# Two decays of a selective scan are computed before the convolution's Silu and kept in a free pair of PSUM banks

## What is computed

```python
xc = silu(conv(xs) + conv_b)                 # per channel, over the tokens
delta = softplus(xc @ xd_w @ dtp_w + dtp_b)
Bm, Cm = xc @ xB_w, xc @ xC_w
dA = exp(delta[..., None] * A)               # the decays
dBx = (delta * xc)[..., None] * Bm[:, :, None, :]
h = dA_t * h + dBx_t                         # step by step over the tokens
y = einsum('bdn,bn->bd', h, C_t) + D * xc
out = y * silu(z) @ out_w + res
```

## Time and profile before

| what | value |
|---|---|
| median of three runs | 10367.23 us (10365.20 to 10386.27) |
| profiled execution | 10389.18 us |
| its span | 10387.4 us |
| mean granted clock of PE | 0.87 of 2.4 GHz |
| DVE busy | 8087.7 us (78% of the span) |
| PE busy | 8344.1 us (80%) |
| POOL busy | 7059.5 us (68%) |
| ACT busy | 5899.2 us (57%) |

### The profile page before, as it was taken

How to read it: one execution, slowest core, us unless ns; L and a number is a source line. 1 busy time by engine, 2 the same in 40 slices (tenths; PEclk the granted TensorE clock), 3 DMA queues, 4 the chain that set the end, 5 groups by cost and what they waited for, 6 DMA issues and landing times. The chain is left out here.

```text
span 10387.4 us, 152898 instructions
## 1 busy us (share of the span) xinstructions
PE 8344.1 (80%) x42776; PEld 6881.5 (66%) x42776; DVE 8087.7 (78%) x10482; ACT 5899.2 (57%) x9202; POOL 7059.5 (68%) x7227
## 2 busy tenths in 40 slices
PE   5877777777878787878787877787877776999998
PEld 4666666666666666666666666676666664777776
DVE  4888889888988888888898888888888894333332
ACT  4565656565665666566566666665566662444443
POOL 4888888888888888888888888888888883000000
PEclk8888888888888888888888888888888887999998
DMA  2222222222222222222222222222222220000000
GB/s 93 94 89 99 92 98 91 99 92 93 92 94 93 90 98 93 90 79 90 89 98 93 98 91 97 93 98 92 90 93 96 92 90 25 11 10 10 12 9 9
DMA packets 414916, 819.68 MB, mean 79 GB/s; under 512 B 148919, under 2 KB 194139, under 8 KB 414043
## 3 DMA queue, kind: packets, MB, share of 16 engines
q1 hardware_dynamic: 410328, 806.69, 22.3%
q10 hardware_dynamic: 3714, 2.89, 0.1%
HBM read 783.16 MB, written 26.30 MB: 78 GB/s over the span
## 5 line engine op out<-in xcount | busy, mean ns | idle before, releaser
L776 ACT ACTIVATE decay<-delta,neg_a 128x512 f32<-128x512 f32 x4096 | 2793.0, 688 | 2484.5 <-DVE h_ps L978 1112.7
L544 POOL TENSOR_TENSOR bu<-b_all,u_buf 128x512 f32<-128x512 f32 x3072 | 3579.4, 1191 | 151.6 <-DVE h_ps L978 148.3
L978 DVE TENSOR_TENSOR_SCAN h_ps<-decay,bu 128x512 f32<-128x512 f32 x2304 | 2782.6, 1222 | 454.6 <-ACT decay L776 376.3
L1233 PE MATMUL y_ps<-ident,ch 128*128 128x128 f32 x16384 | 2579.9, 309 | 637.4 <-DVE ch L998 362.7
L1233 PEld LDWEIGHTS y_ps<-ident,ch 128*128 128x128 f32 x16384 | 2226.7, 161 | 1016.2 <-DVE ch L998 484.4
L556 POOL TENSOR_TENSOR ch<-ch,c_all 128x512 f32<-128x512 f32 x1024 | 1325.5, 1294 | 1112.1 <-DVE ch L978 910.0
L998 DVE TENSOR_TENSOR ch<-h_ps,c_all 128x512 f32<-128x512 f32 x3072 | 1977.2, 671 | 0.0
L547 POOL TENSOR_TENSOR bu<-b_all,u_buf 128x514 f32<-128x514 f32 x1024 | 1245.6, 1237 | 66.8 <-issue 56.3
L1117 PE MATMUL w_ps<-xn,in_w 128*128 128x257 f32 x4096 | 1074.8, 408 | 170.5 <-ACT xn L665 83.6
L982 DVE TENSOR_TENSOR_SCAN h_ps<-decay,bu 128x256 f32<-128x256 f32 x1536 | 1046.7, 737 | 125.3 <-POOL bu L547 98.2
L1117 PEld LDWEIGHTS w_ps<-xn,in_w 128*128 128x128 f32 x4096 | 799.9, 206 | 320.2 <-issue 81.1
(11 more groups left out here) (258 smaller groups left out, 11583.9 us busy)
## 6 DMA issues: line engine op xcount, KB each, us to landing
b_all<-bc_dram SPq DMA_DIRECT2D x512, 514.0 KB, 8.6
c_all<-bc_dram SPq DMA_DIRECT2D x512, 514.0 KB, 10.0
in_w<-in_L_attn_in_w SPq DMA_DIRECT2D x64, 1024.0 KB, 5.0
diag_store<-diag_dram SPq DMA_DIRECT2D x256, 256.0 KB, 2.9
x_in<-in_x SPq DMA_DIRECT2D x128, 256.0 KB, 2.6
out_w<-in_L_attn_out_w SPq DMA_DIRECT2D x64, 512.0 KB, 3.9
skip_diag<-skip_dram SPq DMA_DIRECT2D x64, 256.0 KB, 4.1
h_mid<-h_cur SPq DMA_DIRECT2D x32, 257.0 KB, 2.2
```

What stands on the lines that cost most here:

```text
L544: pool.tensor_tensor(bu[:, s % NBU, 0:NB * L].rearrange("p (b t) -> p b t", b=NB), b_all[:, n // NU, n % NU, :, 1:], u_buf[:, c % 2, :, 1: ...
L776: func(decay[:, s % NDP, :].rearrange("p (b t) -> p b t", b=NB), delta[:, c, :, 1:S], ACT.Exp, scale=neg_a[:, k, c, n:n + 1]).then_inc(dec ...
L978: dve.tensor_tensor_scan(h, decay[:, s % NDP, :], bu[:, s % NBU, 0:NB * L], 0.0, ALU.mult, ALU.add).then_inc(scan_done, 1)
L1233: last = pe.matmul(y_ps[:, k, :], ch[:, s % NPR, k * P:(k + 1) * P], ident[:, :], is_transpose=True, start=False, stop=(n == NST - 1 and k ...
```

## The change

A new key "early" stands between cv3 and xp in the list of results, so it has a slot and two of the three banks of `w_ps`. ACT writes the decays of states 52 and 53 (`EARLY`) into these two banks in unit 24, right behind decay 51 and ahead of `token_rows` and the Silu. The decays of 54 and 55 then wait for the scans of 50 and 51 (`behind`). DVE scans 52 and 53 from those banks and counts "early" as read once scan 53 is done. In the last period, which prepares no job, all is as before.

```diff
+EARLY = 2 * (CONV_AT + 9) + 4, 2 * (CONV_AT + 9) + 5
...
-        steps = first + conv + ["xp", "dt0", "dt1", "dt2", "dt3"]
+        steps = first + conv + ["early", "xp", "dt0", "dt1", "dt2", "dt3"]
...
+            def early_decays(g, jj):
+                k = BLOCK_OF_JOB[jj % 4]
+                w = banks("early", g, jj + 1)
+                for c in (2, 3):
+                    act.wait_ge(read_of(f"cv{c}", g, jj + 1), nth(f"cv{c}", g, jj + 1))
+                for i, s in enumerate(EARLY):
+                    c, n = s // NST, s % NST
+                    func(w[:, i, :].rearrange("p (b t) -> p b t", b=NB), delta[:, c, :, 1:S], ACT.Exp,
+                         scale=neg_a[:, k, c, n:n + 1]).then_inc(decays_ready, 1)
+                act.sem_inc(full_of("early", g, jj + 1), 1)
...
-                if positive(job_count(g, jj, STATES, s + 1 - NDP)):
-                    act.wait_ge(scan_done, job_count(g, jj, STATES, s + 1 - NDP))
+                if positive(job_count(g, jj, STATES, s + 1 - NDP - behind)):
+                    act.wait_ge(scan_done, job_count(g, jj, STATES, s + 1 - NDP - behind))
...
             def lead(g, jj, s, last):
+                if not last and s in EARLY:
+                    return
                 if not (last and s >= STATES):
-                    decays(g, jj, s)
+                    decays(g, jj, s, behind=NDP if not last and s - NDP in EARLY else 0)
...
                     lead(g, jj, NU * u + NDP + 1, last)
+                    if NU * u + 2 * NDP in EARLY and not last:
+                        early_decays(g, jj)
                     if u == silu_at(jj)[1]:
                         token_rows(g, jj, u // PAIRS - 1)
...
+            def decay_of(g, jj, s, last):
+                if s in EARLY and not last:
+                    return banks("early", g, jj + 1)[:, EARLY.index(s), :]
+                return decay[:, s % NDP, :]
...
+            def early_read(g, jj):
+                dve.wait_ge(scan_done, job_count(g, jj, STATES, EARLY[-1] + 1))
+                dve.sem_inc(read_of("early", g, jj + 1), 1)
...
                         c_times_h(g, jj, s)
                         if s + 1 not in POOL_C:
                             c_times_h(g, jj, s + 1)
+                    if s in EARLY and not last:
+                        early_read(g, jj)
```

More of the change, by code:

```diff
@@ L762, in stream_out, with decays @@
                 func(dst[:, c, :, :], w[:, :, 0:S], ACT.Identity).then_inc(read_of(name, g, jj), 1)
-            def decays(g, jj, s):
+            def early_decays(g, jj):
[8 more added lines that the diff above has]
+                act.sem_inc(full_of("early", g, jj + 1), 1)
+            def decays(g, jj, s, behind=0):
                 jj, s = on(jj, s)
@@ L819, in prepare_back @@
                     conv_output(g, jj, c + 1)
+                act.wait_ge(read_of("cv3", g, jj), nth("cv3", g, jj))
+                act.sem_inc(full_of("early", g, jj), 1)
+                act.sem_inc(read_of("early", g, jj), 1)
                 conv_silu(g, jj)
@@ L962, in h_slot, with scan @@
                 return len([v for v in range(s) if v not in POOL_C]) % NU
-            def scan(g, jj, s, b):
+            def decay_of(g, jj, s, last):
[5 more added lines that the diff above has]
+                dve.sem_inc(read_of("early", g, jj + 1), 1)
+            def scan(g, jj, s, b, last):
                 inside = s not in POOL_C
@@ L976, in scan @@
                 if s >= NST:
-                    dve.tensor_tensor_scan(h, decay[:, s % NDP, :], bu[:, s % NBU, 0:NB * L], 0.0, ALU.mult, ALU.add
+                    dve.tensor_tensor_scan(h, decay_of(g, jj, s, last), bu[:, s % NBU, 0:NB * L], 0.0, ALU.mult, ALU.add
                                            ).then_inc(scan_done, 1)
@@ L1055, in period @@
                     for b in range(NB if s < NST else 1):
-                        scan(g, jj, s, b)
+                        scan(g, jj, s, b, last)
                     if u - 1 in y_at(jj):
@@ L1062, in period @@
                         step_size(*size, 0)
-                    scan(g, jj, s + 1, 0)
+                    scan(g, jj, s + 1, 0, last)
                     if s + 1 in POOL_C and s < NST:
                         c_times_h(g, jj, s)
-                        scan(g, jj, s + 1, 1)
+                        scan(g, jj, s + 1, 1, last)
                     else:
                         if s < NST:
-                            scan(g, jj, s + 1, 1)
+                            scan(g, jj, s + 1, 1, last)
                         c_times_h(g, jj, s)
```

## The result

| what | before | after |
|---|---|---|
| median | 10366.22 us (4 runs) | 10444.21 us (4 runs) |
| ratio, 95% interval | | 1.0074 (1.0057 to 1.0092) |
| profiled execution, its span | 10389.18, 10387.4 us | 10442.90, 10441.0 us |

The change makes the kernel 78 us slower (59 to 95 us by the interval).

A forecast was written before the change was run, and what follows sets the result against it. VectorE (87% busy up to 8540 us) was taken to bound the kernel. Weighted by the clock, 0.5 x 2.5 + 0.4 x 0.7 - 0.1 x 1.0 = +1.4 us a job, +88 us over 63 jobs: 10455 us, range 10300 to 10520.

The forecast's parts named there:

- ACT's order: On ScalarE, early decays push y_t, table loads and Silu 1.25 us later; decays 54, 55 end at +5.2, +5.8.
- DVE: On VectorE, scan 52 starts at +0.63, output(2) waits 0.7 us for y2, scan 54 starts 2.6 us earlier.
- The wait for the banks: On TensorE, xp needs the early decays' banks and starts at +4.8, after scan 53, instead of +1.98.
- The rival of a longer wait: The count of "early" waits for product 52, xp starts at +5.4: +2.1 us a job, 10500 us, chance 0.17.
- The Ln as the end of the path: VectorE waits 0.58 us for the first Ln at a job's end; a job gains what that Ln gains.
- The sum with the clock up: With TensorE's clock staying at full rate, the Ln and the job come 1.0 us earlier; 63 jobs gain 65 us.
- The clock: TensorE's clock falls to 1.2 GHz behind idle stretches of 2.25 and 2.3 us, turning the gain into +1.4 us a job.
- The kinds of jobs: Per job: clock stays up -1.0 us; falls only behind second idle stretch +0.7; falls behind the first +2.5.
- The weights: Shares of jobs: one in ten clock up, four in ten fall behind second stretch only, half fall behind the first.
- The clock holds: Rival: TensorE's clock stays up in this stretch, -1.0 us a job, 10302 us, chance 0.15.
- Only xp is hit: Rival: only TensorE's second idle stretch brings the clock's fall, +0.7 us a job, +44 us, 10411 us, chance 0.13.
- The loads for the next job: The store of B and C goes out 0.5 us later, with 7 us of cover before the first reader: costs nothing.

The follow-up runs named there:

- e1: Changed kernel with TensorE given zero-matrix products in both idle stretches, before the skip products and before xp, all waits kept: 10309.92 us, ratio 0.9941.
- e2: Changed kernel with the two early decays in an SBUF buffer and the key "early" removed, so xp waits for the Silu alone: 10274.92 us, ratio 0.9905.
- e6: Changed kernel with only TensorE's second idle stretch, ahead of xp, filled with products that add zeros: 10330.69 us, ratio 0.9958.
- e9: Changed kernel with the key "early" and its bank wait kept, but decays 52 and 53 back in their old place and buffers: 10635.21 us, ratio 1.0260.
- e3: Changed kernel with ScalarE's copy y_t ahead of the two early decays instead of behind them: 10339.98 us, ratio 0.9964.
- e7: e3 with TensorE's adds of states 50 and 51 also moved ahead of xp: 10294.60 us, ratio 0.9924.
- e5: Changed kernel with only TensorE's first idle stretch, before the skip products, filled with zero-matrix products: 10371.45 us, ratio 0.9992.

## Why the prediction was right

- **ACT's order.** y_t, the tables and the Silu 1.25 us later: 1.22 us. Decays 54 and 55 out at +5.8: 4409.82 = +5.76.
- **DVE.** Scan 52 at +0.63: 4404.69 = +0.63. output(2) waits 0.7 us: 0.62. Scan 54 at +5.3: +5.27. DVE is 2.6 us ahead there, and this gain is given back before scan 56, in 2.81 us.
- **The wait for the banks.** xp at +4.8, ended by scan 53 and not by product 52: +4.83. I had left open whether DVE's sequencer passes the product with its count. It does: xp starts at 4408.89, while product 52 (4408.70, 0.67 us) still runs. The rival of a longer wait (10500) fell with that.
- **The Ln as the end of the path.** DVE still waits 0.58 us for it, in the changed kernel as before.
- **The sum with the clock up** was -1.0 us a job and is -0.8. The term that was too small is the dt product's start: on PE the adds of 50 and 51 (1.09 us) stand between xp and it, and it begins 0.8 us after dtbc starts (11.97 against 11.13 us from decay 51 in a job of the first kind), not 0.6, and ends at +10.6 instead of +10.3.
- **The clock** was the step that set the sign, and it held. The kinds of jobs, forecast as -1.0, +0.7 and +2.5 us, are -0.8, +0.9 and 2.3 to 3.0 us. The weights, 0.1, 0.4 and 0.5, are 11, 27 and 25 of 63: 0.17, 0.43 and 0.40. The mean is +1.25 us instead of +1.4, and 63 x 1.25 = 79 us instead of 88. e1 shows that this term, 2.05 us a job, is the clock. That the weights came so near is in part luck: they were drawn from where the clock fell in one job, and with the same 2.22 us the clock fell behind the first stretch in 25 jobs here, in 28 of e2 and in 16 of e6, which the same reasoning had at about half.
- **The rivals.** The clock holds (10302) is what e1 makes of the kernel (10310). Only xp is hit (10411) would have needed the first stretch to be harmless; e6 shows that it isn't. The price of the longer wait was added up a little high: 1.4 + 0.6 is 2.0 us a job, not 2.1.
- **The loads for the next job** did not show: the 10635 us of e9 are explained by 4.2 us a job, though its store goes out still later.

In 52 of the 63 jobs the clock falls behind stretches of 2.22 and 2.40 us, and with both filled in none. The page of the Trainium skill that the prediction weighed (TensorE: Matmul & The Clock Gate, "Why this matters for your kernels") warns only of longer gaps; these runs don't agree with it.

## What to carry to other kernels

A stall's length is not what removing it gives: follow the next operation that the engine must wait for, and see whether the piece moved ahead also stands in front of that one. When a change makes TensorE wait longer, even by a microsecond or two and off the critical path, look at the granted clock of what it runs next; moving ready work of its own into the gap (the two adds) was worth 0.4% (e3 to e7), and swapping two neighbours in ScalarE's queue 1.1% (after to e3), by their ratios to the kernel before. Buffers borrowed from a rotation bring its waits along: whoever writes them next now waits for their last reader.

## What the runs showed of the hardware that was not expected

- A step_size operation of DVE (both inputs in SBUF) took 0.66 to 0.70 us alone. Where it started while a GpSimd instruction ran, it ended 0.55 to 0.64 us behind that one, so it took up to 1.72 us (338 cases in the profile of before). The order of neighbours on DVE decides which of them meets it.
- The clock does not fall behind every idle stretch of a given length: behind 2.8 to 3.0 us it held in 11 jobs of e3 and fell in 52, behind 2.4 us (e5) it fell in 39 of 63. A forecast can only give shares of jobs.
- Products whose result is thrown away, or that add zeros, were enough to hold the clock in all 63 jobs of e1, and gained 1.3% against the same kernel without them.
